# Head 0's maxima of layer 0's attention: two half-row reduces per tile, or a difference, a relu and one fused pass

## The reference

```python
    norm = 1.0 / np.sqrt(KEY_DIM)
    Q = jnp.einsum('bsd,hdk->hbsk', q, W_query)
    K = jnp.einsum('bsd,hdk->hbsk', q, W_key)
    V = jnp.einsum('bsd,hdv->hbsv', q, W_val)
    scores = norm * jnp.einsum('hbqk,hbnk->hbqn', Q, K)
    attn = jax.nn.softmax(scores, axis=-1)
    heads = jnp.einsum('hbqn,hbnv->hbqv', attn, V)
```

## Time and profile before

| | us |
|---|---|
| runs | 1733.25, 1729.99, 1732.26 |
| median | 1732.26 |
| span of the profiled execution, first to last instruction | 1727.5 |
| head 0's maxima, from the first reduce to `negate` | 38.87 to 75.19 |
| DVE busy, share of the span | 75% |
| PE busy, share of the span | 72% |

### The profile page before, as it was taken

How to read it: one execution, slowest core, us unless ns; L and a number is a source line. 1 busy time by engine, 2 the same in 40 slices (tenths; PEclk the granted TensorE clock), 3 DMA queues, 4 the chain that set the end, 5 groups by cost and what they waited for, 6 DMA issues and landing times. The chain is left out here.

```text
span 1727.5 us, 29793 instructions
## 1 busy us (share of the span) xinstructions
PE 1241.6 (72%) x10670; PEld 618.5 (36%) x10674; DVE 1303.3 (75%) x3511; ACT 890.0 (52%) x1757; POOL 235.6 (14%) x275
## 2 busy tenths in 40 slices
PE   7799999999999997575994463060315989823676
PEld 4122222222222223354983342040104556623445
DVE  5999999999999971447237336989898469668783
ACT  4099999999999997312421122020001675612463
POOL 2000000000000000003410314030001321100223
PEclk9599999999999999677995586575656898965668
DMA  2100000001000000000004331000001721022001
GB/s 69 41 10 27 25 20 21 21 26 27 27 21 20 21 3 1 15 30 1 1 1 183 102 86 47 0 0 1 1 1 26 208 70 47 18 101 63 22 22 31
DMA packets 45031, 62.88 MB, mean 36 GB/s; under 512 B 12785, under 2 KB 34357, under 8 KB 44485
## 3 DMA queue, kind: packets, MB, share of 16 engines
q1 hardware_dynamic: 38243, 49.71, 9.7%
q0 software_dynamic: 5440, 10.67, 2.5%
q10 hardware_dynamic: 1200, 0.59, 0.1%
HBM read 34.10 MB, written 13.63 MB: 28 GB/s over the span
## 5 line engine op out<-in xcount | busy, mean ns | idle before, releaser
L842 ACT ACTIVATE l0att_probs<-l0att_ps_sv 128x512 f32<-128x512 f32 x960 | 521.2, 596 | 79.7 <-PE l0att_ps_sv L811 67.9
L888 DVE TENSOR_REDUCE l0att_half_negmax<-l0att_ps_m 128x1 f32<-128x1024 f32 x480 | 547.0, 1215 | 5.3 <-PE l0att_ps_m L741 5.3
L773 PE MATMUL l0att_ps_sv<-l0att_probs,l_V_aug 128*32 128x256 f32 x4096 | 325.3, 392 | 4.8 <-ACT l0att_pv_sb L833 4.7
L811 PE MATMUL l0att_ps_sv<-l_Q,l_K 51*128 51x512 bf16 x992 | 194.4, 388 | 4.0 <-ACT l0att_probs L850 2.4
L741 PE MATMUL l0att_ps_m<-l_K,l_Q 48*128 48x512 bf16 x960 | 185.9, 384 | 11.1 <-DVE l0att_half_negmax L888 7.1
L773 PEld LDWEIGHTS l0att_ps_sv<-l0att_probs,l_V_aug 128*32 128x32 f32 x4096 | 83.0, 108 | 197.1 <-issue 100.5
L811 PEld LDWEIGHTS l0att_ps_sv<-l_Q,l_K 51*128 51x128 bf16 x992 | 48.0, 92 | 207.4 <-ACT l0att_probs L842 188.1
L472 POOL CAST l0att_nm<-l0att_negmax 128x16 bf16<-128x16 f32 x16 | 3.1, 196 | 514.5 <-DVE l0att_negmax L864 514.5
L2862 ACT ACTIVATE l3loc_probs<-l3loc_ps_s 128x320 f32<-128x320 f32 x128 | 48.9, 435 | 36.0 <-PE l3loc_ps_s L2839 35.4
L2040 DVE SCALAR_TENSOR_TENSOR l2spk_lif_v<-l2spk_U 128x64 f32<-128x64 f32 (+1 forms) x368 | 61.6, 211 | 0.0
L2305 PE MATMUL l2spk_ps<-l_X,l2spk_w_terms 128*128 128x512 bf16 x48 | 13.2, 445 | 62.3 <-DVE l_X L2335 62.3
(11 more groups left out here) (736 smaller groups left out, 2392.5 us busy)
## 6 DMA issues: line engine op xcount, KB each, us to landing
l_K<-l_kp SPq DMA_DIRECT2D x192, 32.0 KB
l_Q<-l_qp SPq DMA_DIRECT2D x192, 32.0 KB
l1ffn_W<-in_l_expert_w_dram SPq DMA_DIRECT2D x1, 4096.0 KB
l3f_experts_l_w<-in_l_w_dram SPq DMA_DIRECT2D x2, 2048.0 KB
l_sorted_in<-l1ffn_zeros SPq DMA_DIRECT2D x1, 3072.0 KB
l1exp_rows<-l_sorted_in SPq DMA_DIRECT2D x6, 512.0 KB, 5.6
l_sorted_out<-l1exp_y SPq DMA_DIRECT2D x6, 512.0 KB, 4.6
l_Q<-in_local_mask_q_dram POOLq DMA_DIRECT2D x2, 1170.0 KB, 18.8
```

The costliest lines, as they stand in the source:

```text
L773: mm = pe.matmul(ps_v[32 * c:32 * c + 32, cols], V_aug[:, kt, h, :], probs[:, kt % 2, c, cols], start=(kt == 0 and part == 0), stop=(kt == ...
L811: pe.matmul(dst, K[at, h % HEAD_BUFS, c1(kt)], Q[at, h % HEAD_BUFS, c4(2 * pair + i)], start=True, stop=True).then_inc(last_scored[i] if l ...
L842: act.activation(probs[:, kt % 2, c, :], ps_s[:, n % 3, :], ACT.Exp).then_inc(expd, 1)
L888: dve.tensor_reduce(half_negmax[:, h % 2, t, half:half + 1], src, AX_X, ALU.max, negate=True).then_inc(m_read, 1)
```

## The change

Head 0's maxima are computed in another way. With a the scores of a tile against the first 1024 keys and b those against the last 1024, the larger of each pair is a + relu(b - a). PE makes a as before. It makes b - a directly, as one product over 112 rows: `K_both` holds the last 1024 keys' terms in partitions 0 to 47 and the first 1024 keys' in 64 to 111, `Q_both` holds Q and -Q there, and partitions 32 to 63 of both are cleared first (32 to 47 are then written over). ACT takes the relu into SBUF (`above`). DVE adds `first_low` and `above`, multiplies by -1 and takes the minimum, in one pass per tile (`tensor_tensor_reduce`, two instructions: the pass and the read of its accumulator).

There are now two buffers for a and two for b - a. POOL clears (two memsets), DVE copies (four instructions), and PE's first difference waits for them. SP issues head 1's 24 loads ahead of head 0's 12 high ones instead of behind them. `loaded_first` becomes two semaphores, for Q and K. `negate(0)` reads a single column.

```diff
-        first_scores = [ps_m[:, 0, :], ps_m[:, 1, :], ps_sv[:, 0:2, :].rearrange("p b n -> p (b n)"),
-                        ps_sv[:, 2:4, :].rearrange("p b n -> p (b n)")]
+        first_low = [ps_m[:, 0, :], ps_sv[:, 0:2, :].rearrange("p b n -> p (b n)")]
+        first_diff = [ps_m[:, 1, :], ps_sv[:, 2:4, :].rearrange("p b n -> p (b n)")]
...
             @block.sync
             def _(sp):
-                for piece in high:
-                    load_piece(sp, Q, K, qp, kp, 0, loaded_high, *piece)
                 for h in range(1, L0_H):
...
                     for piece in pieces:
                         load_piece(sp, Q, K, qp, kp, h, loaded[h % HEAD_BUFS], *piece)
+                    if h == 1:
+                        for piece in high:
+                            load_piece(sp, Q, K, qp, kp, 0, loaded_high, *piece)
...
             def _(pool):
+                pool.memset(Q_both[32:64, :], 0.0).then_inc(both_cleared, 1)
+                pool.memset(K_both[32:64, :], 0.0).then_inc(both_cleared, 1)
...
-                pe.wait_ge(loaded_first, LOAD // 2)
-                for n in range(2 * NT):
-                    t, half = n // 2, n % 2
-                    if n >= 4:
-                        pe.wait_ge(first_read, n - 3)
+                for operand in loaded_first:
+                    pe.wait_ge(operand, LOAD // 4)
+                for t in range(NT):
+                    if t >= 2:
+                        pe.wait_ge(first_read, t - 1)
                     for i in range(2):
-                        pe.matmul(first_scores[n % 4][:, i * BANK:(i + 1) * BANK], Q[0:TERMS, 0, c1(t)],
-                                  K[0:TERMS, 0, c4(2 * half + i)], start=True, stop=True).then_inc(first_filled, 1)
-                pe.wait_ge(first_read, 2 * NT)
+                        mm = pe.matmul(first_low[t % 2][:, i * BANK:(i + 1) * BANK], Q[0:TERMS, 0, c1(t)],
+                                       K[0:TERMS, 0, c4(i)], start=True, stop=True)
+                    mm.then_inc(low_filled, 1)
+                    if t == 0:
+                        pe.wait_ge(both_placed, 4)
+                    for i in range(2):
+                        mm = pe.matmul(first_diff[t % 2][:, i * BANK:(i + 1) * BANK], Q_both[:, c1(t)],
+                                       K_both[:, c4(i)], start=True, stop=True)
+                    mm.then_inc(diff_filled, 1)
+                pe.wait_ge(first_read, NT)
...
+                for t in range(NT):
+                    act.wait_ge(diff_filled, t + 1)
+                    if t >= 2:
+                        act.wait_ge(first_read, t - 1)
+                    act.activation(above[:, t % 2, :], first_diff[t % 2], ACT.Relu).then_inc(above_done, 1)
...
-                for n in range(2 * NT):
-                    dve.wait_ge(first_filled, 2 * (n + 1))
-                    dve.tensor_reduce(half_negmax[:, 0, n // 2, n % 2:n % 2 + 1], first_scores[n % 4], AX_X, ALU.max,
-                                      negate=True).then_inc(first_read, 1)
+                dve.wait_ge(both_cleared, 2)
+                dve.wait_ge(loaded_first[1], LOAD // 4)
+                dve.tensor_copy(K_both[0:TERMS, :], K[0:TERMS, 0, S // 2:S]).then_inc(both_placed, 1)
+                dve.tensor_copy(K_both[HALF_ROWS:HALF_ROWS + TERMS, :], K[0:TERMS, 0, 0:S // 2])\
+                   .then_inc(both_placed, 1)
+                dve.wait_ge(loaded_first[0], LOAD // 4)
+                dve.tensor_copy(Q_both[0:TERMS, :], Q[0:TERMS, 0, :]).then_inc(both_placed, 1)
+                dve.tensor_scalar(Q_both[HALF_ROWS:HALF_ROWS + TERMS, :], Q[0:TERMS, 0, :], -1.0, None,
+                                  ALU.mult).then_inc(both_placed, 1)
+                for t in range(NT):
+                    dve.wait_ge(low_filled, t + 1)
+                    dve.wait_ge(above_done, t + 1)
+                    dve.tensor_tensor_reduce(above[:, t % 2, :], first_low[t % 2], above[:, t % 2, :], -1.0, -LOWEST,
+                                             ALU.add, ALU.min, half_negmax[:, 0, t, 0:1]).then_inc(first_read, 1)
```

More of the change, by code:

```diff
@@ L638, in stage_l0_attend @@
         rden = st.sb("rden", [P, 4, NC4])
+        Q_both = st.sb("Q_both", [HALF_ROWS + TERMS, S], BF16)
+        K_both = st.sb("K_both", [HALF_ROWS + TERMS, S // 2], BF16)
+        above = st.sb("above", [P, 2, S // 2])
         ident16 = loads["ident16"]
@@ L658, in stage_l0_attend @@
         nm_placed = [st.sem("nm_placed0"), st.sem("nm_placed1")]
-        first_filled = st.sem("first_filled")
+        both_cleared = st.sem("both_cleared")
+        both_placed = st.sem("both_placed")
+        low_filled = st.sem("low_filled")
+        diff_filled = st.sem("diff_filled")
+        above_done = st.sem("above_done")
         first_read = st.sem("first_read")
@@ L862, in negate @@
                     else:
-                        dve.wait_ge(first_read, 2 * NT)
-                    dve.tensor_tensor(negmax[:], half_negmax[:, h % 2, :, 0], half_negmax[:, h % 2, :, 1],
+                        dve.wait_ge(first_read, NT)
+                    dve.tensor_tensor(negmax[:], half_negmax[:, h % 2, :, 0], half_negmax[:, h % 2, :, min(h, 1)],
                                       ALU.min).then_inc(negmax_ready, 1)
@@ L954, in layer0_attention @@
         ones_placed = st.sem("ones_placed")
-        loaded_first = st.sem("loaded_first")
+        loaded_first = [st.sem("loaded_first_q"), st.sem("loaded_first_k")]
         for half in range(2):
@@ L966, in first_rows @@
                 if (SPLITS_Q, SPLITS_K)[which][r] == part:
-                    load_piece(sp, Q, K, qp, kp, 0, loaded_first, 0, r, which)
+                    load_piece(sp, Q, K, qp, kp, 0, loaded_first[which], 0, r, which)
         stage_project_parts(nc, for_parts, "l0_wqkv", g, 0, "l0proj", V_aug, qp, kp, rows_of_part=first_rows)
```

## The result

| | median | runs | ratio to before, 95% interval |
|---|---|---|---|
| before | 1733.32 us | 20 (1729.86 to 1737.77) | |
| after | 1737.89 us | 20 (1730.50 to 1740.84) | 1.0027 (1.0017 to 1.0037) |

The account below looks back on a forecast made before the run. DVE's reduces were taken to set the pace, so head 0's phase shifts everything behind it. First pass at 44.7, seven turns of 4.29 and the last tile move `negate` from 75.19 to 77.7: 1732.26 + 2.5 = 1734.8 us, range 1728.0 to 1739.5.

Parts of the forecast that it names:

- 0.2% line: Whole kernel: about what a measurement can tell from no change, put at 3.5 us.
- two-input row: Profile row of a two-input DVE pass of 1024 columns, 1.225 us; the fused pass was taken as 1.23 from it.
- rival C: DVE's fused pass (L910) runs at half rate, 2.3 us instead of 1.23: +8.6, 1743.4 us; chance 0.08.
- rival D: Head 0's phase shrinks or grows but the end does not move, something else holding it: 1732.3 us; chance 0.05.
- The order of the loads and the table load: SP's reordered loads and ACT's exp table load behind the last relu: both to cost nothing; load cover 20 us.
- The start: Clears, copies, first difference and relu in series: first fused pass at 44.7, 5.8 us later than the first reduce.
- 0.08 of overlap: DVE's four copies into `Q_both` and `K_both`: 3 x 0.08 us taken off their sum, leaving 2.1.
- A turn: PE's four products, ACT's relu, DVE's pass and hand-offs at half clock: 4.29 us, two tiles in flight, 2.14 per tile.
- Tile 15: Last tile of the phase: its fill queues behind tile 14's on PE, 1.71 us later, and is over at 77.65.
- the stretch behind `negate`: From 75 to 90, after head 0's maxima: moves unchanged with `negate`; about 0.9 us shorter if PE reaches full clock.
- Rival B: PE rises to full clock during the phase: a turn 3.43 us, kernel 1727.9 us; chance 0.27.
- ring: Head 0's chain of PE products, relu and fused pass, two buffers each, replacing DVE's pace: 2.14 us per tile, not 1.15.

Follow-up runs that it names:

- e8_order_only: The kernel before, with only SP's order changed: head 1's 24 loads ahead of head 0's 12 high ones; ratio 0.9987 to before.
- e6_shared: The changed kernel with clears in the stage before and both products of a tile using `Q_both` (112 rows) times `K_both`; one run, -3.1 us against before.
- e4_plain_pass: The changed kernel with a plain reduce of the low scores in place of the fused pass, so other values follow; one run, +26.0 us against before.
- e10_before_112: The kernel before, with head 0's first products on operands of 112 rows, rows 48 to 111 zeros; +3.5 to +10.6 us against before.
- e7_shared_waits: The changed kernel with early clears, looser PE waits, four `above` buffers and 112-row operands for all first products; 1719.72 us, ratio 0.9922 to before.
- e9_before_twice: The kernel before, with each of head 0's first products made twice, all on 48 rows; one run, +20.2 us against before.
- e1_waits: The changed kernel with PE's difference first, waiting only for the relu two tiles back, and four `above` buffers; -2.6 to +3.6 us against before.
- e3_low_twice: The changed kernel with each low product made twice, six products per tile instead of four; +7.1 to +15.9 us against before.
- e2_clear_early: The changed kernel with POOL's two clears moved to the start of the projection stage; -0.9 to +6.8 us against before.
- e5_waits_early: The changed kernel with early clears, looser PE waits and four `above` buffers together; ratio 0.9988 to before.

## Why the prediction was right in kind and short in size

I predicted +2.5 us (1734.8) with a range of 1728.0 to 1739.5. The measured +4.6 puts the kernel within the range (1737.89) and, at 0.27%, on the slower side of the 0.2% line, to which I gave 0.27 of the chance; I had held it likelier (0.57) that it stays within that line.

**Right: the mechanism and the steps that carry it.** The fused pass is 1.225 us, as the two-input row said; rival C is out. DVE waits for ACT before each pass; passes come in pairs, 1.9 and 2.6 apart where I gave 1.7 and 2.6. The clock is 0.50 throughout. Nothing in the steady state absorbs the shift; rival D is out. The order of the loads and the table load cost nothing (e8_order_only; the first exp keeps its 9.54).

**Mis-sized: the start, the turn and the last tile.** `negate` came at 42.2 behind the block's start where I had 40.0. Step by step:
- *The start, 7.0 given, 7.5 measured.* 0.2 of this is no error of the sum: POOL starts with SP, as I had it (36.09 and 36.08), and the whole block lies 0.2 behind the mark in this trace. The copies take 2.31, not 2.1: durations were about as taken (0.42 and 0.69), but I took off 0.08 of overlap for each, and here they don't overlap (38.81, 39.26, 39.71). The rest, 0.1, is the hand-off from ACT to DVE.
- *A turn, 4.29 given, 4.49 measured, times 7 = 1.4.* From PE's start to the end of the difference pair it is 46.70 - 44.71 = 1.99, not 1.89: between pairs of different rows there is 0.53 and not 0.43 from product to product, and e6_shared takes just this away. From ACT's end to DVE's start it is 0.14 and not 0.04, which I had taken over from PE to ACT. e4_plain_pass shows 0.11 with the plain reduce.
- *Tile 15 follows tile 14 by 1.94, not 1.71*, for the same changes between 48 and 112 rows: 0.2.

In sum 0.5 + 1.4 + 0.2 = 2.1 to 2.2, which closes the gap of +2.5 to the +4.7 of the trace. I had written that each 0.1 on a hand-off is +0.8; both slips in the turn were of that size, and both went the same way. The one on PE, the change of rows, had no term in the sum at all.

**Missed: the clock behind the phase.** I took the stretch behind `negate` as rigid. It is so up to the first exp, but a mean of 0.72 over 90 to 100 means 5.6 us at 0.50 and a rise at 95.6, 17.5 behind `negate`; before it is 0.6 us and 90.6, 15.4 behind, and 0.9 more is lost by head 2. What decides this instant I didn't isolate. It isn't shown to belong to the change: over the traces of all thirteen kernels the rise lies 15.0 (e8_order_only) to 20.0 us (e10_before_112) behind `negate`, though the work there is the same, and up to head 2 the shift grows by about half of what the rise is late (0.9 for 2.1 in after, 2.0 for 4.6 in e10_before_112). So of the 5.6 us of this trace 4.7 are the phase, and 0.9 go with where the rise fell in the one execution that was profiled.

**Rival B was right about the turn, and its condition was not the one I argued.** A turn at full clock is 3.53, the 3.43 that I gave and 0.1 of the hand-off. The stretch behind `negate`, which B had 0.9 shorter, is not: the clock falls back there, and the first exp comes 9.52 behind `negate` in e6_shared and 9.31 in e7_shared_waits, against 9.54. I gave 0.27 to a rise of the clock, for 80% against 75% busy, and argued against it with the gap in each tile. The gap wasn't what kept it down: with PE busy without any gap the clock stayed 0.50 for 48 rows (e9_before_twice) and for 48 and 112 in turn (e1_waits, e3_low_twice). It rose only in the four kernels in which all first products have 112 rows, one trace each, and in one of them, e10_before_112, only for 7 us; so the rows are a part of the condition and not the whole. The Trainium skill (TensorE: Matmul & The Clock Gate, "Part 1: The HAM clock gate (the "warmup" mystery)") says that sustained matmul work releases the clock; in e9_before_twice the 30 us of it shown above did not, and here the measurement decides.

**Where the halved DVE work went.** In three places, each shown by taking it away: 2.6 to 2.9 to the clears (e2_clear_early), 5.5 to 5.7 to waiting for the wrong event (e1_waits), and 8.0 (33.8 to 25.8, e5_waits_early and e7_shared_waits) to PE's four products per tile at half clock with their changes of rows. Half clock and changes of rows weren't taken away singly; my sum for even rows at half clock was 32.5, so by that estimate most of the 8.0 is the clock. With all three gone `negate` is 25.8 behind the block's start instead of 37.5, and the time 13.5 us less than before (11.3 to 15.6).

## What to carry to other kernels

When work is moved off the busiest engine, count the waits of the chain that takes its place: with two buffers, time per tile is half the chain's length, and each buffer should be freed by its own reader, not by the last one in the chain. A hand-off that is taken as 0.04 and is 0.14 costs as often as the chain turns, so take it from a row between the same two engines. And before a ring's price is settled at half clock, ask which products TensorE runs there: here the same arithmetic in wider operands, with zeros in them, was worth 8 us of the phase where PE set the pace. Where DVE set it, the wider operands of e10_before_112 cost 3.5 to 10.6 us, so it is worth a try only where PE is the bound.

## What the runs showed of the hardware that was not expected

- Products on 48 rows, busy for 30 us without a gap, left the granted clock at 0.50; with 112 rows it rose to 1.00 (e9_before_twice, e6_shared), for 7 us also with 64 of the rows zeros in both operands (e10_before_112). There it fell again with PE busy for 3.03 of 5 us, and stayed at 0.50 with PE busy for 16.46 of 18 us on 112 rows. Rows are not all it takes.
- A change between products of 48 and of 112 rows costs 0.11 per pair; between pairs of 112 rows nothing is seen, whether the weights are the same or those of another tile (0.96 against 0.85 and 0.86 from pair to pair, after and e6_shared).
- In these traces DVE's short SBUF copies overlap when the output of both starts at the same partition, and not when it changes between partitions 0 and 64. In after every copy changes it: 0.42 long, 0.45 apart; 0.69 long, 0.72 apart. In e6_shared the first two copies of K both write from partition 0 and are 0.34 apart, the third writes from 64 and is 0.44 behind the second:

```profile
36.82 0.42 DVE L894 COPY l_K_both<-l_K 48x1024 bf16<-48x1024 bf16 x1 [3.16 <-PEq L509]
37.16 0.41 DVE L895 COPY l_K_both<-l_K 48x1024 bf16<-48x1024 bf16 x1
37.60 0.42 DVE L896 COPY l_K_both<-l_K 48x1024 bf16<-48x1024 bf16 x1
```

In e10_before_112 two copies of 2048 columns, both to partition 0 on, are 0.61 apart with 0.69 of length. The input starts at partition 0 in all of them. So the 0.08 of overlap that the prediction took off fits copies that write from the same partition, and not the order of these four. Two fused passes overlap too, 1.225 long and 1.15 apart (e7_shared_waits).
